# Up projection of a gated, quantised MLP block: from plain block products to Strassen's scheme on one Trainium2 core

## The reference

```python
# x (2, 2048, 512), cond (2, 128); D = 512, FF = 2048, BN = 128
scale = cond @ norm_w.T + 1.0
h = x * (scale[:, None, :] * rsqrt(mean(x * x, -1) + 1e-6))
val, gate = split(h @ up_w.T, 2, -1)              # up_w (4096, 512)
h = val * gelu(gate)
y = act_quant(h) @ weight_quant(down_w).T          # 127 levels by the token's max |h|; weights -1, 0, 1
x1 = y + x
dWd = ((cond @ Wdd.T + bdd) * 0.1).reshape(B, BN, D)   # Wdd, Wdu: (65536, 128)
dWu = ((cond @ Wdu.T + bdu) * 0.1).reshape(B, D, BN)
out = x1 + relu(x1 @ (Wd + dWd).T + bd) @ (Wu + dWu).T + bu
```

## Time and profile before

| what | value |
|---|---|
| time, median of 3 runs | 945.19 us (944.78 to 945.75) |
| span of the profiled execution, first to last instruction | 943.8 us |
| PE busy | 917.3 us, 97% of the span, 4328 matmuls |
| DVE busy | 591.9 us, 63% |
| ACT busy | 190.2 us, 20% |
| POOL busy | 23.9 us, 3% |
| DMA | 110.02 MB, 117 GB/s over the span |

### The profile page before, as it was taken

The page is one execution under the profiler, slowest core; times in us unless marked ns, Lnnn a source line. Parts: engine busy times, 40 slices in busy tenths (PEclk is TensorE's granted clock), DMA queues, the critical chain, the costliest instruction groups (busy, mean ns, idle before and its releaser), DMA issues.

```text
span 943.8 us, 10872 instructions
## 1 busy us (share of the span) xinstructions
PE 917.3 (97%) x4328; PEld 393.8 (42%) x4328; DVE 591.9 (63%) x907; ACT 190.2 (20%) x298; POOL 23.9 (3%) x33
## 2 busy tenths in 40 slices
PE   2999999999999999999999999999999999999998
PEld 1333433344333443444434444444444444444443
DVE  3888689738644484454944369554774559453795
ACT  2445421222112111121111221121101211111000
POOL 0000000000000000000000000000000000000000
PEclk9999999999999999999999999999999999999999
DMA  7377737632355315433173332020101100020012
GB/s 256 128 280 268 258 124 243 252 136 92 130 186 181 127 57 203 159 136 136 46 269 137 136 107 75 1 90 32 59 1 44 45 1 1 1 90 0 1 70 108
DMA packets 37026, 110.02 MB, mean 117 GB/s; under 512 B 4080, under 2 KB 4080, under 8 KB 36976
## 3 DMA queue, kind: packets, MB, share of 16 engines
q1 hardware_dynamic: 35952, 108.28, 32.3%
q10 hardware_dynamic: 1024, 1.05, 0.4%
HBM read 96.73 MB, written 11.53 MB: 115 GB/s over the span
## 4 chain that ended last, share of the span: by engine, by line
PE 94%; DVE 3%; issue 2%; POOL 0%; ACT 0%; DVEq 0%; POOLq 0%
PE up_ps L549 23%; PE up_ps L550 23%; PE up_ps L551 23%; PE aux_ps L613 10%; PE aux_ps L584 6%; PE aux_ps L648 3%; PE aux_ps L639 3%; PE up_ps L624 1%; DVE work L837 1%; PE aux_ps L594 1%; PE aux_ps L603 0%; DVE qscale L850 0%; DVE x_lo L797 0%; POOL work L417 0%; PE aux_ps L655 0%
## 5 line engine op out<-in xcount | busy, mean ns | idle before, releaser
L549 PE MATMUL up_ps<-x_hi,u_hi 128*128 128x512 f16 x1024 | 389.2, 380 | 4.7 <-issue 2.0
L551 PE MATMUL up_ps<-x_hi,u_lo 128*128 128x512 f16 x1024 | 388.6, 379 | 0.0
L550 PE MATMUL up_ps<-x_lo,u_hi 128*128 128x512 f16 x1024 | 388.6, 379 | 0.0
L819 DVE SCALAR_TENSOR_TENSOR h_sb<-up_ps,unscale,gelu 128x512 f32<-128x512 f32 x128 | 95.9, 750 | 301.1 <-PE up_ps L551 297.1
L510 ACT ACTIVATE gelu<-up_ps,unscale 128x512 f32<-128x512 f32 x128 | 87.9, 686 | 595.1 <-PE up_ps L551 587.8
L549 PEld LDWEIGHTS up_ps<-x_hi,u_hi 128*128 128x128 f16 x1024 | 100.7, 98 | 166.6 <-issue 47.7
L551 PEld LDWEIGHTS up_ps<-x_hi,u_lo 128*128 128x128 f16 x1024 | 100.3, 98 | 121.2 <-issue 0.7
L550 PEld LDWEIGHTS up_ps<-x_lo,u_hi 128*128 128x128 f16 x1024 | 100.4, 98 | 114.0 <-issue 2.9
L613 PE MATMUL aux_ps<-q_sb,wq 128*128 128x512 f16 x448 | 97.9, 379 | 0.6 <-issue 0.5
L837 DVE TENSOR_REDUCE work<-h_sb 128x512 f32<-128x2048 f32 x24 | 88.5, 3689 | 0.3
L858 DVE TENSOR_TENSOR h_sb<-h_sb,qscale 128x512 f32<-128x512 f32 x128 | 86.7, 682 | 0.4
(11 more groups left out here) (69 smaller groups left out, 374.5 us busy)
## 6 DMA issues: line engine op xcount, KB each, us to landing
w_ring<-in_Wdd SPq DMA_DIRECT2D x64, 512.0 KB, 4.6
w_ring<-in_Wdu SPq DMA_DIRECT2D x64, 512.0 KB, 4.2
out<-x_sb SPq DMA_DIRECT2D x9, 1024.0 KB, 4.9
q_sb<-in_up_w SPq DMA_DIRECT2D x16, 512.0 KB, 6.1
x_sb<-in_down_w SPq DMA_DIRECT2D x16, 512.0 KB, 5.4
x_sb<-in_x SPq DMA_DIRECT2D x7, 1024.0 KB, 8.3
x_sb<-out SPq DMA_DIRECT2D x3, 1024.0 KB, 5.6
out<-x_sb SPq DMA_DIRECT2D x8, 256.0 KB, 2.0
```

The costliest lines, as they stand in the source:

```text
L549: pe.matmul(ps, whi, xhi, start=(k == 0), stop=False)
L550: pe.matmul(ps, whi, xlo, start=False, stop=False)
L551: mm = pe.matmul(ps, wlo, xhi, start=False, stop=(k == KD - 1))
L819: dve.scalar_tensor_tensor(out=h_sb[:, j, :], in0=up_ps[2 * (p % 2) + 1][:, :], scalar=unscale[:, BATCH[i], j:j + 1], in1=gelu[:, p % 2, : ...
```

## The change

Two blocks of 512 tokens make a superblock (`TS` = 1024), of which there are 4. A step for both blocks at once is called a quad here; there are 64 (`NQ`), 16 per superblock. The quad's product is a 2 x 2 by 2 x 2 block product: (value, gate) rows by (first, second half of the 512 input features), times those halves by (first, second 512 tokens). It is done with 7 block products in place of 8, in the Winograd form, products numbered 1 to 7. Each has 2 chunks of three matmuls. Sums of the weights are formed on GpSimd, sums of the tokens on GpSimd (on DVE for the first superblock), and the sums of the products by copying PSUM banks (ACT `seed_b`, `keep_p5`) and adding (DVE `seed_c`, `val2`), partly by accumulating more products into the same bank. The 7 weight blocks no longer stay on chip: they are written to DRAM in superblock 0 and read back for every quad of superblocks 1 to 3 (`put_e`, `put_l`, `load_e`, `load_l`; 384 and 512 KB a quad). The auxiliary PSUM banks go from four to two. The running maximum is kept quad by quad (ACT takes the absolute value, DVE the maximum). The residual input is read again from DRAM, and blocks 0 to 5 go through DRAM between residual and adapter. The program's core, cut:

```diff
-        u_hi = sb("u_hi", [P, NP, KD, UW], F16)
-        u_lo = sb("u_lo", [P, NP, KD, UW], F16)
+        u_e = sb("u_e", [P, 2, 2, 768], F16)
+        u_l = sb("u_l", [P, 2, 2, 1024], F16)
+        t_mov = sb("t_mov", [P, 7, 2, 2 * TB], F16)
+DW_QUADS = ((2, 0), (16, 8), (51, NG))
+ASSEMBLE = 52
+QUANTISE = {2: 3, 3: 3, 4: 2, 5: 2, 6: 2, 7: 2, 8: 2}
+Y_FIRST = 9
+MID_AT = {53: 0, 55: 1, 61: 2}
+def side_work(n):
+    s, j = divmod(n, NP)
+    work = [("dw", g) for g in groups_of_quad(n)]
+    if s + 1 < NSB:
+        if j in (5, 6):
+            work.append(("stat", 2 * s + 2 + j - 5))
+        if j in (7, 8):
+            work.append(("rs", 2 * s + 2 + j - 7))
+    if s > 0 and Y_FIRST <= j < Y_FIRST + 4:
+        for m in (2 * (j - Y_FIRST), 2 * (j - Y_FIRST) + 1):
+            work.append(("y", 2 * (s - 1) + m // KD, m % KD))
...
         @block.sync
+            for n in range(NQ):
+                s, j = divmod(n, NP)
+                if s == 0:
+                    put_e(j)
+                    put_l(j)
+                    if j + 3 < NP:
+                        load_u(j + 3)
+                    if 1 <= j <= 8:
+                        load_d(j - 1)
+                if NP <= n + 2 < NQ:
+                    load_e(n + 2)
+                if NP <= n + 1 < NQ:
+                    load_l(n + 1)
+                for g in groups_of_quad(n + 1):
+                    if g >= 2:
+                        load_w(2 * g)
+                        load_w(2 * g + 1)
+                if s == 1 and j < 8:
+                    load_d(8 + j)
+                if j == 2:
+                    load_x(s + 1)
...
+            def load_d(n):
+                if 1 <= n < 9:
+                    sp.wait_ge(s_dabs, n)
+                elif n >= 9:
+                    sp.wait_ge(s_wq, n - 8)
+                sp.dma_start(d_raw, down_w[n % 8]).then_inc(s_d, 16)
...
         @block.gpsimd
+            def sums_e(j):
...
+                s1 = s_sum(0).rearrange("p (k m) -> p k m", k=2)
...
+                pool.tensor_tensor(s1, a_block(j, 0, 0), a_block(j, 1, 0), ALU.add)\
+                    .then_inc(s_us, 1)
...
+            def add_squares(i):
+                for k in range(1, KD):
+                    pool.wait_ge(s_sq, KD * i + k + 1)
...
+                    pool.tensor_tensor(res[:, 2, :], res[:, 2, :], res[:, 3, :], ALU.add)\
+                        .then_inc(s_sqp, 1)
+            def t_late(s):
+
+                pool.wait_ge(s_tlo, 7 * s + 2)
+                pool.wait_ge(s_t_sum, 4 * (s - 1) + 2)
+                pool.tensor_tensor(t_sum(T2), t_sum(T3), t_sum(B11), ALU.add).then_inc(s_t_sum, 1)
...
         @block.scalar
+            def squares(i):
...
+                for k in range(KD):
+                    if k > 1:
+                        act.wait_ge(s_sqp, (KD - 1) * (i - 2) + k - 1)
+                    act.activation(res[:, 2 + (k > 0), :], x_sb[:, i % 2, k, :], ACT.Square)\
+                        .then_inc(s_sq, 1)
...
+            for n in range(NQ):
+                s, j = divmod(n, NP)
+                last = j == NP - 1 and s + 1 < NSB
+                if n:
+                    for g in groups_of_quad(n - 1):
+                        stage_group(g)
...
+                    if j == 0:
+                        t_high(s, T3)
+                    seed_b(n)
+                    if last:
+                        t_high(s + 1, B11)
+                    keep_p5(n)
+                    if last:
+                        t_high(s + 1, T1)
+                    gate2(n - 1)
+                    if last:
+                        t_high(s + 1, T2)
+                    if j == 0:
+                        t_high(s, B22)
+                    absolute2(n - 1)
+                    absolute1(n - 1)
+                if s == 0 and j + 1 < NP:
+                    u_high(j + 1, 2)
+                    u_high(j + 1, 3)
+                if s > 0 and j == 0:
+                    t_high(s, T4)
+                gate1(n)
+                if last:
+                    t_high(s + 1, B21)
+                if s == 0 and j + 2 < NP:
+                    u_high(j + 2, 0)
+                    u_high(j + 2, 1)
+                if s == 0 and 1 <= j <= 8:
+                    down_abs(j - 1)
+                if s + 1 < NSB and j in (5, 6):
+                    squares(2 * s + 2 + j - 5)
...
         @block.tensor
+            for n in range(NQ):
+                product(n, 1)
+                product(n, 5)
+                if n:
+                    product(n - 1, 3)
+                product(n, 6)
+                if n:
+                    product(n - 1, 4)
+                product(n, 2)
+                product(n, 7)
+                for key in side_work(n):
...
+            product(NQ - 1, 3)
+            product(NQ - 1, 4)
+            adapter_mid(3)
+            adapter_mid(4)
+            for i in (3, 4):
+                for k in range(KD):
+                    adapter_up(i, k)
...
+            for c in range(NP):
+                last_down(0, c, banks)
+                if c == 9:
+                    adapter_mid(5)
+                if c == 11:
+                    for k in range(KD):
+                        adapter_up(5, k)
...
+            for c in range(NP):
+                last_down(1, c, banks)
+                if c == 4:
+                    adapter_mid(6)
+                if c == 6:
+                    for k in range(KD):
+                        adapter_up(6, k)
+            adapter_mid(7)
+            for k in range(KD):
+                adapter_up(7, k)
...
         @block.vector
+            for n in range(NQ):
+                s, j = divmod(n, NP)
+                last = j == NP - 1 and s + 1 < NSB
+                if n:
+                    for key in side_work(n - 1):
+                        if key[0] == "y":
+                            residual(key[1], (key[2],))
+                        elif key[0] == "rs":
+                            x_scaled(key[1])
...
+                if n:
+                    multiply2(n - 1)
+                seed_c(n)
+                if n:
...
+                    multiply1(n - 1)
+                    running_max2(n - 1)
+                    running_max1(n - 1)
...
+                if s + 1 < NSB and j == 7:
+                    ins = rsqrt(s + 1, slice(0, 2 * NT), 2 * s + 4)
+                    ins.then_inc(s_rs, 2)
+                if s == 0 and j + 2 < NP:
+                    u_max(j + 2)
+                if s > 0 and j == 1:
+                    dve.wait_ge(s_ma, 2 * s)
+                    step(s - 1, slice(0, TS))
+                    inverse(slice(0, 256))
+                    inverse(slice(256, 512))
+                val2(n)
...
+                if s == 0 and j + 1 < NP:
+                    u_low(j + 1, 2)
+                    u_low(j + 1, 3)
+                if s == 0 and j + 2 < NP:
+                    u_scale(j + 2)
+                    u_low(j + 2, 0)
+                    u_low(j + 2, 1)
...
+                if s > 0 and j in QUANTISE:
+                    first = sum(v for q, v in QUANTISE.items() if q < j)
+                    quantise(s - 1, range(first, first + QUANTISE[j]))
+                if s == 1 and j < 8:
+                    down_quantise(j)
+                if n == ASSEMBLE:
+                    assemble()
```

More of the change, by code:

```diff
@@ L43 @@
 NB = B * S // TB
-BATCH = [i * TB // S for i in range(NB)]
 KD = D // P
@@ L112, in aux_plan @@
[L112 to L131 removed]
+B11, T1, T2, B21, T3, B22, T4 = range(7)
@@ new lines, with slot_tables @@
+MOVING = {1: B11, 5: T1, 6: T2, 2: B21, 7: T3, 3: B22, 4: T4}
+def slot_tables():
+    order, spare, packed = [list(range(NP))], [list(range(NP, NP + 5))], []
+    for s in range(NSB):
+        o, sp = order[s], spare[s]
+        packed.append([sp[4]] + o[0:7])
+        order.append(sp[0:4] + o[7:16] + [sp[4]] + o[0:2])
+        spare.append(o[2:7])
+    return order, packed
+ORDER, PACKED = slot_tables()
+SLOTS = NP + 5
+U_SLOT = (16, 17, 18)
+SUM_SLOT = 19
+DW_QUADS = ((2, 0), (16, 8), (51, NG))
@@ L132, in aux_plan, with mid, up @@
+def aux_plan():
+    def mid(i):
+        return [("mid", i)]
+    def up(i):
+        return [("up", i, k) for k in range(KD)]
+    uses = [("scale", 0), ("stat", 0), ("stat", 1), ("rs", 0), ("rs", 1)]
+    for n in range(NQ):
+        uses += side_work(n)
+    uses += mid(3) + mid(4) + up(3) + up(4) + mid(5) + up(5) + mid(6) + up(6) + mid(7) + up(7)
     return {key: n for n, key in enumerate(uses)}
@@ L533, in _ @@
+            gate2(NQ - 1)
+            absolute2(NQ - 1)
+            absolute1(NQ - 1)
+            for i in range(3, NB):
+                adapter_relu(i)
         @block.tensor
@@ L988, in _ @@
-            i = NB - 1
-            q_product(i, 0)
+            n = NQ - 1
+            for key in side_work(n):
+                if key[0] == "up":
+                    finish(key[1], key[2])
+            multiply2(n)
+            multiply1(n)
+            running_max2(n)
+            running_max1(n)
```

(23 more changed lines are left out.)

1220 lines of the change are left out of this document (717 added, 503 removed).

## The result

| | before | after |
|---|---|---|
| median | 945.18 us (944.78 to 945.75, 4 runs) | 1202.38 us (1201.24 to 1205.3, 4 runs) |
| span of the profiled execution | 943.8 us | 1201.1 us |
| PE busy | 917.3 us, 97% | 913.6 us, 76%, 3950 matmuls |
| mean granted TensorE clock | 1.000 | 0.872 |

A forecast was written before the change was run, and what follows sets the result against it. The prediction took PE's own work to bound the kernel before. It summed start 64.6, superblock 0 200, superblocks 1 to 3 655 and tail 82.7 to 1002.3, 1004 us with 1.4 around the span; range 978 to 1030.

The forecast's parts named there:

- tail: After the last product 4: DVE leads while PE waits in pieces; 82.7 us, 20 of it added idle time.
- the price of GpSimd's sums: GpSimd additions, unseen in the profile: 1.13 us per 512 elements, taken from `affine_select` at 2.2 ns an element.
- the clock among the rivals: PE idling in pieces lowers its clock: 15 to 20 us at worst; 1036 us, chance 0.18 shared with GpSimd contention.
- the stalls in superblocks 1 to 3: PE waits for squares, d load, superblock changes and superblock 3's steps: 54 to 56 us atop 599 of work.
- The load of d: Superblock 1, quads 0 to 7: `down_quantise` waits for d, queued behind w loads on SP; 26 us.
- The squares: Superblock 2: PE reaches `stat` before the squares are summed, 5 us twice; 12 us with `rsqrt` and the reciprocal quad.
- The changes of superblock: ACT's high parts and GpSimd's token sum delay `seed_b`: 4.2 us after superblock 0, 8 for the two later changes.
- a loop of ACT and DVE: Superblock 0: ACT passes DVE-fed instructions before `seed_b`, so an ordinary quad takes 10.2 us where PE needs 9.07.
- GpSimd in DVE's way: Rival: GpSimd additions, 79 us, block DVE for four tenths of that time; 1036 us, chance 0.18 shared with the clock.
- The streams bind: Rival: superblocks 1 and 2 move about 3.0 MB a quad, too much at 241 GB/s; 1035 us, chance 0.10.
- PE stays fed: Rival: queues run ahead, removing nine tenths of 109 us of middle stalls; 906 us, chance 0.12.
- the 17 and the 24 us: Unknown ends: squares' GpSimd additions at 2.1 us add 17; loads at 241 GB/s add 24 over 8 quads.

The follow-up runs named there:

- e9: e8 with the adapter groups' copies behind `seed_b` on ACT in all of superblock 0: 979.89 us, ratio 1.038 to the kernel before.
- e1: The changed kernel with the four weight additions a quad on DVE instead of GpSimd: 1099.92 us, ratio 1.1637.
- e2: The changed kernel with weight sums left on GpSimd, its reduction over partitions of the weights' maxima replaced by a one-element addition: 1100.54 us, one run.
- e0: The kernel before with small GpSimd additions, reductions and fills added in three idle stretches: 945.15 us; each change between addition and reduction cost 6.0 to 9.9 us.
- e5: e1 with 28 unread matmuls on PE ahead of each wait for the squares, to keep the clock up: 1102.21 us.
- e8: e7 with two late token sums per superblock change on DVE and `seed_b` ahead of ACT's token and group copies in the first quad: 987.98 us.
- e6: e1 with squares spread later, d loaded ahead of w, superblock 0's square additions on DVE, first two adapters a quad later: 1037.74 us, ratio 1.0982.
- e7: e6 with `u_high` parts 0 and 1 behind `gate2` and their low parts behind `seed_c` in superblock 0: 1005.21 us, ratio 1.0633.

## Why the prediction was wrong in size

Stage by stage, in us, against the forecast (e9 has the mended orders; e1 has the changed kernel's, but for the sums):

| stage | forecast | after | e1 | e9 |
|---|---|---|---|---|
| to product 6 of quad 1 | 64.6 | 89.3 | 67.5 | 62.8 |
| superblock 0, to product 6 of quad 16 | 200 | 313.6 | 229.7 | 174.5 |
| to the last product 4 | 655 | 709.2 | 708 | 653 |
| tail | 82.7 | 89.1 | 89.1 | 89.1 |

Slower was right; the miss is 198.8 us of span, 24.7 + 113.6 + 54.2 + 6.4 by stage.

**The step that failed: the price of GpSimd's sums.** The prediction said "No row shows GpSimd adding", took 1.13 us an addition of 512 from a row of time per element, and gave the sums of the weights no term of their own; the change of kind was priced at nothing. The rows were on the desk: the reduction of the earlier trace rows has 8.45 us of "issue" ahead of it and the `affine_select` of the earlier trace rows, from which the price was taken, 8.7. I read the durations and not the brackets. It is 106 of the 199 us: 22 at the start, 84 in superblock 0 (e1; by e2 17 and 84, with one change left at the start). The Trainium skill has a sentence that would have led there: GPSIMD Engine Reference, Instruction dispatch, says that the first call of a freshly loaded GpSimd program pays a code load of about 6 us without an instruction in the profile. The 6.0 to 9.9 us of e0 are in line with it; the `MODIFY_POOL_CONFIG` pair at the head of each gap agrees too. That code is loaded in these gaps no run shows.

**The second: PE's work at full clock.** The sum costed every matmul at 0.216 and put the clock among the rivals at "15 to 20 us at worst". By the busy times, before's 917.3 less the 82.9 taken out would be 834; it was 914. By stage PE was busy for 180.5 us in superblock 0 where the forecast had 147 of work, 634.7 for 599 in superblocks 1 to 3, 70.2 for 62 in the tail: 77 in all. This is not to be added to the first term: 16 of the 33 us in superblock 0 went with the gaps (164.7 in e1). The mean durations of the float16 groups, with 0.38 at full and 0.63 at half clock, make some 280 matmuls at half clock; 280 x 0.21 is about 60 us (an estimate). The float32 products of the adapters have another 10 (67.0 us for 56.8). The rest may be the modelled ends ahead of the many gaps, which was not tried. This term falls with the stalls: e9 has 870, at a mean clock of 0.956.

**The third: the stalls in superblocks 1 to 3.** Idle there: 709.2 - 634.7 = 74.5, forecast 54 to 56. The load of d was right in mechanism and near in size (26 forecast; 26.7 of DVE's wait, and 22 off superblock 1 when removed). The squares were 5 us a piece in the forecast; in the changed kernel quads 37 and 38 took 20.6 and 20.5 us, where quad 39, which has none, took 11.8. The additions of 512 elements took 1.44 on average, not 1.13, and ACT and GpSimd pass the buffer back and forth:

```profile
746.77 1.50 POOL L540 TENSOR_TENSOR res<-res 128x512 f32<-128x512 f32 x1 [14.62 <-ACT res L623]
749.01 1.46 POOL L540 TENSOR_TENSOR res<-res 128x512 f32<-128x512 f32 x1 [0.74 <-ACT res L623]
751.21 1.53 POOL L540 TENSOR_TENSOR res<-res 128x512 f32<-128x512 f32 x1 [0.74 <-ACT res L623]
```

```profile
752.89 1.84 PE L879 MATMUL aux_ps<-ones,res 128*128 128x1 f32 x8 [6.60 <-POOL res L540]
```

The idle row says 6.6 us, near the 5 forecast plus three additions 0.3 longer each; the other 2 us of the 9 fit PE's slower clock behind the wait, which e5's quad 38 shows at 2.3 in two products and 0.8 in `stat`. The changes of superblock were forecast 4.2 longer each; e8 took 4.6 to 5.5 off them.

**What held.** PE has its 384 matmuls fewer: a late quad of the loop with two y sums takes 16.0 us, which is 42 x 0.216 = 9.07 and 6.9 for y. Superblock 0 is a loop of ACT and DVE with `seed_b` last ahead of product 6, and once the changes of kind are gone it takes 229.7 against 200. PE's slower work there is 17.7 us (164.7 for 147); whether it lies on the loop, so that 12 are left, is not shown. The tail had 18.9 us idle for 20.7.

**The rivals.** *GpSimd in DVE's way* is real (e6's pair), and not what was missed: with the 64 additions beside DVE (e2) or on it (e1) superblock 0 takes 229.2 or 229.7 us. What the meeting costs by itself these two do not separate, as e1 pays for the additions on DVE. *The streams bind*: superblocks 1 and 2 moved 206 and 205 GB/s, e9 240 in a shorter superblock 1. The chain has DMA at 4%, 3% of it d, an order. DVE's longest DMA wait, 50.1 us for the x of the residual, is not on it. So this rival fell. *PE stays fed* fell for the kernel as written. Its case against, waits by program order, was right, and from e1 to e9 120 us go, by moving lines and by two more pieces of GpSimd's work on DVE (e6, e8). Even so PE idles 109 us of e9's span for 26.5 before, which is 82 more, while its busy time is only 47 us shorter (870.4 for 917.3), not 83: together the 35 us. On the range: the prediction's own ends do not add up, as the 17 and the 24 us that it names above 1004 give 1045, not 1030.

**What stays open.** Whether the start (62.8 us to product 6 of quad 1, 32.8 of them idle on PE; before's first 66 us have 20.3 idle) and the tail (89.1 us, 19.3 idle; before's last 58.5 have 3.3) can be had back by order alone. No run was aimed at them: e1 took 22 us off the start and e7 3, from e7 to e9 the start varies between 62.8 and 66.3 without an edit to it, and the tail took 86.5 us in e6 and e8, at a granted clock of 0.94 for 0.90, likewise without one. If both had only before's idle time, e9 would take some 951 us (979.9 - 12.5 - 16.0, an estimate), still no gain; 57 of the 109 idle us are in the superblocks. That leaves the scheme undecided in principle.

## What to carry to other kernels

Give each engine's queue a price for changing the kind of work, not only for the work; on GpSimd keep either additions or reductions over partitions in a loop, unless the engine would wait longer anyway where it changes, as on the way back here; and read the idle time in the brackets of even one-off rows. A saving on the engine that bounds is worth nothing until its feeders have the slack: here 83 us of matmuls less left PE idle for 287.5 us in place of 26.5, and cost clock as well. When work leaves the critical engine, write down for each instruction that feeds it what stands ahead of it in its own queue; of what was written down so here, the load of d, the squares of superblocks 1 and 2, the changes of superblock and the tail came within 1 to 7 us each, while the loop of superblock 0 measured 30 us more than forecast even without the changes of kind.
